# Layer 0's scores by heads in 32-column tiles of TensorE, in a fused two-layer attention kernel

## What is computed

```
# layer 0, per sample; x, y: [256, 2048], 8 heads of 32 channels
q = Wq @ y + bq; k = Wk @ y + bk; v = Wv @ x + bv
scores = einsum('hdl,hel->hde', q, k) / 16        # 32x32 for each head
out = einsum('hde,hel->hdl', softmax(scores), v)
o = Wo @ out + bo + x
x1 = (o - mean(o)) * rsqrt(var(o) + eps) * gn_w + gn_b
# layer 1: q, k, v from y; softmax within chunks of 64 positions; + x1; instance norm
```

## Time and profile before

| what | value |
|---|---|
| time, median of 3 runs | 1567.83 us (1567.61 to 1570.94) |
| the profiled execution, its own time | 1568.77 us |
| its span in the trace | 1566.7 us |
| PE busy | 1541.8 us, 98% |
| DVE busy | 1339.6 us, 86% |
| ACT busy | 1000.0 us, 64% |
| POOL busy | 458.0 us, 29% |
| granted TensorE clock | 0.996 of full |

### The profile page before, as it was taken

The page is one execution under the profiler, slowest core; times in us unless marked ns, Lnnn a source line. Parts: engine busy times, 40 slices in busy tenths (PEclk is TensorE's granted clock), DMA queues, the critical chain, the costliest instruction groups (busy, mean ns, idle before and its releaser), DMA issues.

```text
span 1566.7 us, 53872 instructions
## 1 busy us (share of the span) xinstructions
PE 1541.8 (98%) x23828; PEld 1304.0 (83%) x23828; DVE 1339.6 (86%) x2027; ACT 1000.0 (64%) x1805; POOL 458.0 (29%) x294
## 2 busy tenths in 40 slices
PE   9999999999999999999999999999999999999995
PEld 7888888888888888888888888888888888888884
DVE  5778888898898888988889888888889889888897
ACT  5656665666656667566675765766666665666655
POOL 1114233142331414214142241423314233141331
PEclk9999999999999999999999999999999999999998
DMA  7132341424314243232423415234142331424121
GB/s 254 54 96 76 110 123 36 149 79 120 110 58 135 75 131 95 82 118 68 142 83 101 124 44 151 86 98 125 45 149 77 122 110 55 134 80 127 58 70 67
DMA packets 96392, 157.22 MB, mean 100 GB/s; under 512 B 5408, under 2 KB 38304, under 8 KB 96032
## 3 DMA queue, kind: packets, MB, share of 16 engines
q1 hardware_dynamic: 96160, 153.78, 31.7%
HBM read 120.20 MB, written 33.55 MB: 98 GB/s over the span
## 4 chain that ended last, share of the span: by engine, by line
PE 96%; DVE 2%; DMA 1%; issue 0%; ACT 0%; SPq 0%; ACTq 0%; POOL 0%; POOLq 0%; DVEq 0%
PE pj_ps L312 46%; PE l_ps L312 12%; PE s_ps L336 7%; PE w_ps L347 7%; PE l_ps L432 7%; PE w_ps L365 6%; PE s_ps L325 3%; PE l_ps L450 2%; PE l_ps L470 2%; PE l_ps L458 1%; PE l_ps L464 1%; PE l_ps L452 1%; PE l_ps L473 1%; DMA y_raw<-in_ctx 1%; DVE o_sb L949 0%
## 5 line engine op out<-in xcount | busy, mean ns | idle before, releaser
L1103 POOL TENSOR_TENSOR prob<-prob,row_inv 128x1024 f32<-128x1024 f32 x128 | 262.4, 2050 | 919.6 <-DVE row_inv L846 919.6
L661 ACT CAST att_hi<-w_ps 128x256 fp32r<-128x256 f32 x256 | 82.9, 376 | 244.6 <-PE w_ps L365 237.9
L312 PE MATMUL pj_ps<-y_hi,w_hi 128*128 128x512 f32 x510 | 206.7, 405 | 0.0
L312 PE MATMUL pj_ps<-y_hi,w_lo 128*128 128x512 f32 x510 | 201.3, 395 | 0.0
L312 PE MATMUL pj_ps<-y_lo,w_hi 128*128 128x512 f32 x510 | 201.2, 395 | 0.0
L841 DVE TENSOR_REDUCE row_sum<-prob 128x16 f32<-128x1024 f32 x128 | 154.9, 1210 | 53.0 <-ACT prob L643 53.0
L829 DVE TENSOR_REDUCE row_max<-s_ps 128x16 f32<-128x1024 f32 x128 | 155.8, 1217 | 20.1 <-PE s_ps L336 17.6
L638 ACT COPY prob_t<-w_ps 128x512 f32<-128x512 f32 x256 | 149.8, 587 | 19.6 <-PE w_ps L347 16.8
L1120 POOL TENSOR_TENSOR o_sb<-o_sb,u_sb 128x1024 f32<-128x1024 f32 x60 | 157.9, 2643 | 2.7 <-ACT o_sb L651 2.7
L814 DVE TENSOR_TENSOR yt_hl<-yt_raw,yt_hl 128x1024 fp32r<-128x1024 f32 x64 | 119.8, 1871 | 42.8 <-ACT yt_hl L606 40.8
L836 DVE TENSOR_TENSOR prob<-s_ps,row_max 128x1024 f32<-128x1024 f32 x128 | 155.2, 1213 | 0.1
(11 more groups left out here) (141 smaller groups left out, 3593.6 us busy)
## 6 DMA issues: line engine op xcount, KB each, us to landing
y_raw<-in_ctx SPq DMA_DIRECT2D x64, 512.0 KB, 4.9
yt_raw<-in_ctx_t SPq DMA_DIRECT2D x64, 512.0 KB, 4.6
x_raw<-in_x SPq DMA_DIRECT2D x64, 512.0 KB, 5.2
out_z<-o_sb SPq DMA_DIRECT2D x60, 512.0 KB, 3.6
mask_b<-in_mask SPq DMA_DIRECT2D x64, 256.0 KB, 4.0
out_z<-o_sb SPq DMA_DIRECT2D x8, 256.0 KB, 2.7
u_sb<-in_w SPq DMA_DIRECT2D x2, 512.0 KB, 5.8
w_sb<-in_w SPq DMA_DIRECT2D x1, 1024.0 KB, 10.3
```

Source lines behind the costliest of these rows:

```text
L312: last = mm(dst, lhs, rhs, start=i == 0, stop=i == len(todo) - 1)
L1103: nc.gpsimd.tensor_tensor(cut, cut, row_inv[:, u % 2, :].unsqueeze(2).to_broadcast([P, 2 * HEADS, CHUNK]), ALU.mult).then_inc(probs_done, 1)
```

## The change

Two products of layer 0 are cut to what is used of them.

- **Scores.** In place of four matmuls of 128x128 by 128 columns (L458), PE issues 16, one for each head and each half of the 256 contracted channels, with 128x32 weights, 32 moving columns, and its output in the 32 partitions of its own column strip. The result is kept compact: `a0` is [128, 2, 32], each head's 32x32 block in its own 32 partitions.
- **Broadcast product.** In place of two matmuls with 256 moving columns in slot 7 (L452), 16 of the same small form in slot 8, ahead of the scores. `y_sum_b` and `v_row` shrink to 32 columns a half; `bk_l` is laid out the same way once, at the start, by four ACT instructions in place of one.
- **DVE.** `v_row` is made in slot 8 instead of 7. The mask add is gone, and the bias add, the maximum and ACT's exponents work on 32 columns a half. The division is split: `layer0_inverse` (the reciprocal) stays in slot 9, and `layer0_normalize` moves to slot 10, between `att_low` and `shift`. There it writes `a0_wide`, the block diagonal matrix, from compact `a0`, the reciprocal and a mask of ones and zeros, in two instructions. The mask is made from the old one at the start, by one DVE instruction.
- **Statistics of z.** The pair of instructions of slot 6 (`stats_of_z`) moves to slot 7, beside the pair that is there.

```diff
                 elif s == S_T1:
                     pe.wait_ge(gram_done, count(n, 1, 0))
-                    pe.wait_ge(y_sum_done, count(n, 1, 0))
...
-                    for k in range(HALVES):
-                        last = mm(l0_ps[0][:, 0:E], y_sum_b[:, k, :], w0_sb[:, K_W, k, :], start=k == 0, stop=k == 1)
                     last.then_inc(t1_ready, 1)
                 elif s == S_SC:
+                    pe.wait_ge(y_sum_done, count(n, 1, 0))
                     pe.wait_ge(t1_done, count(n, 1, 0))
                     for i in range(HALVES):
                         for k in range(HALVES):
-                            last = mm(l0_ps[0][:, i * P:(i + 1) * P], w0_sb[:, Q_W, k, i * P:(i + 1) * P], t1[:, k, i * P:(i + 1) * P],
-                                      start=k == 0, stop=k == 1)
+                            for h in range(4):
+                                o = i * P + DH * h
+                                mm(l0_ps[0][DH * h:DH * h + DH, P + i * DH:P + (i + 1) * DH], y_sum_b[:, k, :], w0_sb[:, K_W, k, o:o + DH],
+                                   start=k == 0, stop=k == 1)
+                    for i in range(HALVES):
+                        for k in range(HALVES):
+                            for h in range(4):
+                                o = i * P + DH * h
+                                last = mm(l0_ps[0][DH * h:DH * h + DH, i * DH:(i + 1) * DH], w0_sb[:, Q_W, k, o:o + DH], t1[:, k, o:o + DH],
+                                          start=k == 0, stop=k == 1)
                     last.then_inc(sc0_ready, 1)
...
-            def layer0_normalize(n):
+            def layer0_inverse(n):
                 dve.wait_ge(a0_exp, count(n, 1, 0))
                 nc.vector.reciprocal(a0_sum[:, :], a0_sum[:, :]).then_inc(a0_step, 1)
+
+            def layer0_normalize(n):
                 dve.wait_ge(a0_step, count(n, 4, 3))
-                tt(a0[:, :, :], a0[:, :, :], a0_sum[:, :].unsqueeze(2).to_broadcast([P, HALVES, P]), ALU.mult).then_inc(a0_done, 1)
+                for i in range(HALVES):
+                    last = stt(out=a0_wide[:, i, :].rearrange("p (h c) -> p h c", h=4), in0=a0[:, i, :].unsqueeze(1).to_broadcast([P, 4, DH]),
+                               scalar=a0_sum[:, i:i + 1], in1=head_mask.rearrange("p (h c) -> p h c", h=4), op0=ALU.mult, op1=ALU.mult)
+                last.then_inc(a0_done, 1)
...
+                        if s == S_U:
+                            layer0_normalize(n)
...
                     if s == S_SC + 1:
-                        layer0_normalize(n)
+                        layer0_inverse(n)
```

More of the change, by code:

```diff
@@ L114, in build @@
         gram = u0 = work_b
-        v_row = sb("v_row", [P, E])
-        a0 = sb("a0", [P, HALVES, P])
+        v_row = sb("v_row", [P, HALVES, DH])
+        a0 = sb("a0", [P, HALVES, DH])
+        a0_wide = sb("a0_wide", [P, HALVES, P])
         a0_max = sb("a0_max", [P, HALVES])
@@ L463, in layer0 @@
                     for i in range(HALVES):
-                        last = mm(l0_ps[1][:, i * E:(i + 1) * E], a0[:, i, :], w0_sb[:, O_W, i, :], start=True, stop=True)
+                        last = mm(l0_ps[1][:, i * E:(i + 1) * E], a0_wide[:, i, :], w0_sb[:, O_W, i, :], start=True, stop=True)
                     last.then_inc(u0_ready, 1)
@@ L718, in _ @@
             act.wait_ge(w0_in, 2 * 16)
-            nc.scalar.mul(bk_l[:, :], bk_row[:, :], float(L)).then_inc(consts_done, 1)
+            for h in range(4):
+                rows = slice(DH * h, DH * h + DH)
+                last = nc.scalar.mul(bk_l[rows, :, :], bk_row[rows, :].rearrange("p (i o) -> p i o", i=HALVES)[:, :, rows], float(L))
+            last.then_inc(consts_done, 1)
             def body(n, first, last):
@@ L874, in layer0 @@
                     for i in range(HALVES):
[L875 to L877 removed]
+                        last = stt(out=t1[:, i, :], in0=bk_row[:, :], scalar=y_sum[:, i:i + 1], in1=l0_ps[1][:, i * E:(i + 1) * E],
+                                   op0=ALU.mult, op1=ALU.add)
+                    last.then_inc(t1_done, 1)
                 elif s == S_SC:
                     dve.wait_ge(sc0_ready, count(n, 1, 0))
[L880 removed]
+                    tt(v_row[:, :, :], l0_ps[0][:, P:P + HALVES * DH].rearrange("p (i o) -> p i o", i=HALVES), bk_l[:, :, :],
+                       ALU.add).then_inc(a0_step, 1)
+                    dve.wait_ge(a0_step, count(n, 4, 0))
                     for i in range(HALVES):
[L882 to L883 removed]
+                        last = stt(out=a0[:, i, :], in0=v_row[:, i, :], scalar=col[:, V_BQ0, i:i + 1],
+                                   in1=l0_ps[0][:, i * DH:(i + 1) * DH], op0=ALU.mult, op1=ALU.add)
                     last.then_inc(a0_step, 1)
[L885 to L886 removed]
                     dve.wait_ge(a0_step, count(n, 4, 1))
@@ L1029, in body @@
                         flags(n, b + 1)
-                    if not first and T_Z_STATS <= s < T_Z_STATS + BLOCKS:
+                    if not first and s != S_SUM and T_Z_STATS <= s < T_Z_STATS + BLOCKS:
+                        if s == S_SUM + 1:
+                            stats_of_z(n - 1, S_SUM - T_Z_STATS)
                         stats_of_z(n - 1, s - T_Z_STATS)
```

15 lines of the change are left out of this document (8 added, 7 removed).

## The result

| | before | changed |
|---|---|---|
| time, median of 6 runs each | 1570.80 us | 1559.51 us (1557.83 to 1563.14) |
| ratio | | 0.9938, 95% interval 0.9926 to 0.9950 |
| profiled execution, its own time | 1568.77 us | 1557.83 us |
| its span | 1566.7 us | 1556.0 us |

The changed kernel is faster by 0.62% (0.50 to 0.74%), about 9.7 us. The two medians alone differ by more, 11.3 us, since the six runs of before lie in two groups, 1567.6 to 1567.8 and 1570.7 to 1570.9 us. The forecast was a gain of 10.6 us, to 1557.2 us. The size is near; it is not made up as forecast. One term was left out, and three others (a record, the edges, the new wait in slot 10) turned out smaller than taken.

A forecast was written before the change was run, and what follows sets the result against it. It took PE's stream to bound the kernel: 1.77 us removed, 0.99 added and 0.12 of new wait a sample, times 16, give 10.6 us off, from 1567.83 to 1557.2 us; range 1551.5 to 1567.0 us.

The forecast's parts named there:

- a record: Slot 8: each of the 64 records of small matmuls costs 10.2 ns start to start, 0.65 us a sample.
- the edges: Slot 8: going into the tiled form costs 0.09 us and coming out 0.25, together 0.34 us a sample.
- the new wait in slot 10: Slot 10: PE's weight load for the product with Wo waits for the later a0_wide, 0.12 us a sample.
- Slot 7, removed: Slot 7: taking out the broadcast product L452 frees 0.87 us of PE a sample, all on the path.
- what the moved statistics cost in their new place: Slot 7: the pair of statistics moved from slot 6 makes t1 no later, so it costs nothing.
- The section: Slot 8: the small matmuls with their ways in and out add 0.65 + 0.34 = 0.99 us a sample.
- Rival C: Slot 8: full-height column strips take turns at 28 ns a record, 7.7 us slower, 1575.5 us; chance 0.11.
- the point of decision: Slot 8: from 20 ns a record on, strips taking turns decides the outcome.
- The floor of about 25 ns: Slot 8: the skill's least start-to-start time for any matmul; by it 1.60 us, the kernel 4.6 us slower, 1572.5.
- this delay dies out: Behind slot 10's division: shift comes 0.60 us later on DVE, absorbed by its waits for PE at slot starts.
- The sum: Whole kernel: PE's savings less additions and the wait give 0.66 us a sample, 10.6 us over 16 samples.

The follow-up runs named there:

- e_z6: The changed kernel with the pair of statistics of z back in slot 6; one run, 1570.49 us, against 1568.68 us for the kernel before.
- e_strips: The changed kernel with the same 64 records reordered, so that all matmuls of one column strip follow one another; one run, 1571.08 us.
- e_pre9: The changed kernel with VectorE's reciprocal and widening of layer 0 in slot 9, ahead of the reciprocal that releases GpSimd's scaling; 1553.55 us, ratio 0.9900 to before.
- b_div10: The kernel before, with only its wide division moved from slot 9 to slot 10; 1574.00 us against 1568.60, ratio 1.0032.
- e_norm9: The changed kernel with the widening division back in slot 9, right behind the reciprocal; 1556.97 us, ratio 0.9927 to before.
- both swaps: The changed kernel with VectorE making o_bias ahead of the previous sample's result in slot 11: in all samples 1557.27 us, in all but the last 1554.27 us.
- e_norm9tt: The changed kernel with the division in slot 9 behind the reciprocal, made of two tensor-by-tensor operations of 64 and 256 columns; one run, 1554.14 us.

## Why the prediction was right, and where it was not

**Slot 7, removed: right.** 0.87 us forecast, 0.89 measured. But the prediction asked only what the moved statistics cost in their new place (nothing, as it said). It did not ask what came late in slot 7 once PE was there 0.87 us sooner. `branch` was the answer, and only the move kept it off the path [e_z6]. The forecast held here thanks to a part of the change that it had priced at nothing.

**Slot 8, records and edges: right in kind, both somewhat too dear.** 64 records at 10.2 ns were 8.5; the edges, taken at 0.34 us, were 0.29. The section, forecast at 0.99 us, took 0.85. To take the edges from slot 10's rows, as an own term, was right: without them the sum would have been 0.29 x 16 = 4.6 us too good. The Trainium skill's rule in TensorEngine Tiling (Array Packing), Key Properties, that a change of tiling mode drains the engine, agrees with these 0.29 us; that it is a drain, no run shows.

**Rival C: not in this order.** The strips do run at once at full height. In e_strips, in which neighbours share one, a record cost 20.5 ns, at the point of decision, and the gain was gone. The floor of about 25 ns that the prediction cites from TensorE: Matmul & The Clock Gate of the Trainium skill holds for neither: 8.5 and 20.5 ns.

**Slot 10, the new wait: right in kind, smaller.** 0.12 us forecast, 0.06 measured; `a_wide` took 0.61 us, within the 0.60 to 0.69 forecast. It shows as a later weight load and not, as forecast, as 16 waits in the list; that it goes when the widening leaves slot 10 is shown by e_pre9 (12.44).

**Slot 12: the step that failed.** The prediction said of the 0.60 us by which the widening puts off all that stands behind it on VectorE: "DVE waits for PE at the start of each such slot (0.92 us in slot 10), so this delay dies out". There is slack at slot 10, ahead of the new work, but none between it and slot 12: VectorE runs without a gap from `att_lo` to `o_bias`, partly since the result's two operations take 2.58 us there, as they did before the change. The delay arrives at `o_bias` almost whole, 0.44 us a sample. b_div10 shows it without the rest of the change (0.35 us for 0.42 us of work), e_pre9, e_norm9 and both swaps take it away in three different ways. One slot's idle time had been taken for that of all.

**The sum.** By the forecast 0.87 + 0.90 - 0.99 - 0.12 = 0.66 us a sample; measured 0.89 + 0.05 - 0.06 - 0.44 = 0.43. The missed 0.44 was partly made good by the section's 0.14, the wait's 0.06 and 0.02 in slot 7. Over the whole execution it came nearer still, since two samples are without the wait in slot 12 (7.8 us by the slots, against 10.6 forecast), and since the stray delays of the two profiled executions differ by some 2.6 us, which nobody forecast. That the total came so near is luck: errors of opposite sign met.

## What to carry to other kernels

When work is moved on an engine that is not the bottleneck, follow its timeline from the new place to the next operation that the bottleneck wants, and look for a gap on that stretch; idle time ahead of the new place or the engine's mean load doesn't help. When work is taken from the bottleneck, ask what it covered: here a statistic had to make way, or three quarters of the gain in that slot would have been a wait. Small matmuls in column strips pay when neighbours in the program sit in different strips and all of them stand in one stretch; a further stretch cost 0.29 us a sample here.

## What the hardware showed that I had not expected

- **Who is held is not told by the start of the record.** The kernel before had one tensor-by-tensor operation (L917) behind `row_inv`: its mean was 0.424 us, and GpSimd's scaling, which started 0.02 us behind it, took 2.16 us for 1.90. In e_norm9, at the same place beside the same scaling by GpSimd, an operation with a per-partition scalar began at 163.08, GpSimd's at 163.10, and the pair took 2.33 us, the first of it 2.07. Both are so in all 16 samples. So the Trainium skill's rule cited above, that the first to start wins, did not hold by the records' starts for this form; it did for e_norm9tt's tensor-by-tensor operation (0.23 us), and for the second one, which started later and was held. Why the form matters, no run shows.
- **A smaller copy gained nothing.** The spreading of the sum (L911, 256 columns, and L921, 64 columns) stands beside GpSimd's addition. It fell only from 2.03 to 1.93 us, median of 16. The least, 194 ns (295 before), is the first sample's, in which no addition is beside it:

```profile
L921 DVE COPY y_sum_b<-y_sum x16: 194/1925/1929, 52.5 to 1481.2; 128x64 f32<-128x64 f32 x16
```

- **Column strips of full height stream at once,** f32 with 32 moving columns: 8.5 ns a record when interleaved, 20.5 ns when not.
- **The same stretch of the last sample ran at either clock level.** In the changed kernel TensorE stood idle for 1.77 us ahead of it and the granted clock was 1.00; in e_pre9 it stood idle for 1.73 us, and for 0.22 us more just ahead of it, and the clock was 0.50 for 3.1 us. What decided it isn't shown.
